# Routing the older chunks of attention sooner, and turning the last chunk's first image later

## The reference

```python
t = _to_tokens(x)
t = t + _L1_attn_ref(_ln_t(t), ...)
t = t + _L1_ffn_ref(_ln_t(t), ...)

# attention, 8 searches of width 16, 2 retrievals
search_attn = softmax(einsum('bsid,bsjd->bsij', sq, sk))
retrieved = einsum('bsij,brjd->bsird', search_attn, rv)
rk = retrieved @ wk_ret
retrieval_attn = softmax(einsum('bsid,bsird->bsir', rq, rk))
out = einsum('bsir,bsird->bsid', retrieval_attn, retrieved)   # then @ w_out

# experts, 8 of them, each token goes to its 2 best
router_logits = einsum('bsd,de->bse', x, Wg)
top_logits, top_idx = top_k(router_logits, 2)
top_w = softmax(top_logits)
out = out + cw[:, e:e + 1] * (silu(xt @ W1[e]) @ W2[e])       # summed over e
```

## Time and profile before

| | |
|---|---|
| runs | 669.68, 670.31, 671.67 us, median 670.31 |
| profiled execution | 670.67 us |
| its span from first to last instruction | 668.9 us |
| PE, DVE, ACT, POOL busy | 565.4, 474.3, 333.6, 262.1 us |
| mean granted clock of PE | 0.924 |

### The profile page before, as it was taken

One profiled execution on the slowest core, in us unless ns is written; L12 is line 12 of the kernel. 1 busy time (PEld: TensorE's weight loads), 2 busy tenths in 40 slices (PEclk: granted clock), 3 DMA queues, 4 the chain that ended last, 5 costly groups with the idle time before them and its releaser, 6 DMA issues. The chain is left out here.

```text
span 668.9 us, 10706 instructions
## 1 busy us (share of the span) xinstructions
PE 565.4 (85%) x3180; PEld 438.6 (66%) x3180; DVE 474.3 (71%) x1227; ACT 333.6 (50%) x718; POOL 262.1 (39%) x328
## 2 busy tenths in 40 slices
PE   5999999939878999999999997884199999999910
PEld 4788888727655776767676765553078888888800
DVE  6796775756467778888888797876357676776716
ACT  3321412124446555565646464552178888888700
POOL 3245344539100010141413232357504666666660
PEclk9999999968969999999999997987579999999975
DMA  8994144649731403142323223001397777786009
GB/s 268 355 371 143 65 159 161 193 159 391 212 110 48 143 16 127 33 132 59 126 65 106 87 87 105 18 32 41 96 340 241 227 242 239 238 248 212 36 9 367
DMA packets 55224, 105.46 MB, mean 158 GB/s; under 512 B 8744, under 2 KB 21689, under 8 KB 55040
## 3 DMA queue, kind: packets, MB, share of 16 engines
q1 hardware_dynamic: 49040, 94.93, 43.0%
q0 software_dynamic: 4992, 8.54, 3.6%
q10 hardware_dynamic: 1136, 1.31, 0.8%
HBM read 58.15 MB, written 48.42 MB: 159 GB/s over the span
## 5 line engine op out<-in xcount | busy, mean ns | idle before, releaser
L1978 POOL DMA_INDIRECT y_slots<-virt,pad_l x92 | 95.9, 1043 | 73.2 <-DVE virt L2030 50.1
L1304 DVE TENSOR_REDUCE s_max<-bank 128x2 f32<-128x512 f32 x128 | 85.9, 687 | 24.3 <-PE bank L1627 23.6
L1069 ACT ACTIVATE s_expd<-bank 128x512 f32<-128x512 f32 x128 | 76.9, 602 | 48.8 <-PE bank L1648 47.8
L983 POOL DMA_INDIRECT x_slots<-rows,slot_of x64 | 62.4, 976 | 67.4 <-DVE rows L1435 49.8
L2018 DVE TENSOR_TENSOR k_stack<-virt,k_stack 128x512 fp32r<-128x512 f32 x92 | 63.5, 690 | 25.5 <-ACT k_stack L1997 24.8
L947 POOL TENSOR_TENSOR ln_rstd<-ln_var,power 128x4 f32<-128x4 f32 x17 | 17.4, 1026 | 146.7 <-DVE ln_var L1280 146.6
L1663 PE MATMUL bank<-s_expd,rvx 128*64 128x256 f32 x512 | 71.7, 402 | 1.6 <-ACT s_expd L1069 1.1
L61 PE MATMUL bank<-pad_h,u_h 128*128 128x512 f32 x144 | 59.4, 412 | 9.4 <-DVE pad_l L399 8.2
L1648 PE MATMUL bank<-q_stack,k_stack 100*128 100x256 f32 x256 | 61.8, 324 | 5.2 <-DVE q_stack L1322 5.0
L1997 ACT ACTIVATE k_stack<-virt 128x512 fp32r<-128x512 f32 x92 | 58.2, 633 | 10.5 <-PE bank L63 8.0
L1992 ACT ACTIVATE virt<-bank 128x512 f32<-128x512 f32 x92 | 55.1, 598 | 14.5 <-PE bank L63 14.3
(11 more groups left out here) (260 smaller groups left out, 1321.2 us busy)
## 6 DMA issues: line engine op xcount, KB each, us to landing
x_slots<-blank SPq DMA_DIRECT2D x8, 2112.0 KB, 17.3
pad_h<-w_split SPq DMA_DIRECT2D x23, 512.0 KB, 4.1
q_stack<-w_split SPq DMA_DIRECT2D x23, 512.0 KB, 5.8
qk_rows<-qk SPq DMA_DIRECT2D x15, 512.0 KB, 3.1
k_stack<-qk_rows SPq DMA_DIRECT2D x96, 64.0 KB, 2.5
pad_l<-x_slots SPq DMA_DIRECT2D x23, 264.0 KB, 5.1
q_stack<-qk_rows SPq DMA_DIRECT2D x42, 128.0 KB, 2.5
e_raw<-in_w SPq DMA_DIRECT2D x16, 256.0 KB, 2.9
```

The costliest lines, as they stand in the source:

```text
L983: pool.indirect_dma_start(out=x_slots[:, :], out_offset=bass.IndirectOffsetOnAxis(ap=slot_of[:, ring, k, j:j + 1], axis=0), in_=rows[:, ri ...
L1069: nc.scalar.activation(expd[:, s % 4].rearrange("p a i -> p (a i)"), ps_st[s % 2][:, :], ACT.Exp).then_inc(exp_done, 1)
L1304: nc.vector.tensor_reduce(s_max[:, :, s], banks[s % len(banks)][:, :].rearrange("p (a j) -> p a j", a=2), AX.X, ALU.max).then_inc(max_done, 1)
L1978: pool.indirect_dma_start(out=y_slots[:, :], out_offset=bass.IndirectOffsetOnAxis(ap=ids, axis=0), in_=y_rows[:, t % 2, j, :], in_offset=N ...
```

## The change

Nothing that is computed changes, only the order of work in the bodies of g = 6 and g = 7. On DVE, the third routing part of chunk 4 and the statistics of chunk 5 go behind the first half of body 6; chunk 4 is ranked and placed within its second half; chunk 5 is routed at the end of it instead of in body 7, and placed in the first half of body 7. Chunk 6 is turned back and routed by PE one head sooner, and routed on DVE between the retrieval parts of the last chunk's image A. PE turns image A at head 7 and makes its output product behind the last retrieval. ACT's copies follow. On POOL, chunk 5's scatters go around the rstd of chunk 6, and three scatters of chunk 6 instead of one go ahead of the rstd of image A.

```diff
 # POOL
         for g in range(1, NCH):
+            if g == NCH - 1:
+                scatter(g - 2, 1, (0,), (0, 1))
             rstd(tail_norm(g - 1))
+            if g == NCH - 1:
+                scatter(g - 2, 1, (0,), (2, 3))
+                scatter(g - 2, 1, (1,))
             copy_rows(g - 1, (g - 1) % 2)
             if g + 2 < NCH:
                 rstd(2 * g + 2)
-            if g >= 2:
+            if g >= 2 and g < NCH - 1:
                 scatter(g - 2, g % 2)
-        scatter(NCH - 2, 0, (0,), (0,))
+        scatter(NCH - 2, 0, (0,), range(0, 3))
         rstd(tail_norm(IMAGE_A))
-        scatter(NCH - 2, 0, (0,), range(1, G))
         pool.wait_ge(scattered[1], 2 * G * 16 * (NCH // 2 - 1))
         number_rows(NCH - 1, 1)
-        scatter(NCH - 2, 0, (1,), (0,))
+        scatter(NCH - 2, 0, (0,), range(3, 4))
+        scatter(NCH - 2, 0, (1,), range(0, 3))
         rstd(tail_norm(IMAGE_B))
-        scatter(NCH - 2, 0, (1,), range(1, G))
+        scatter(NCH - 2, 0, (1,), range(3, 4))
 # ACT, body: share_exp; last_body: share_exp, keep_z2, keep_logits, keep_o
-                    if s == 4 and g >= 2:
+                    if g >= 2 and s == (4 if stage == MIDDLE else 1):
                         share_exp(g - 2)
...
+                if s == 1:
+                    share_exp(g - 2)
                 if s == 2:
                     gate(g - 1, 1)
                 if s == 4:
                     keep_o(g - 1)
-                if s == 6:
-                    share_exp(g - 2)
...
+                if s == 1:
+                    keep_z2(g - 1)
                 if s == 2:
                     gate(g, 0)
-                    keep_z2(g - 1)
-                if s == 4:
                     keep_logits(g - 1, 0)
                 if s == 6:
+                    share_exp(g - 1)
+                if s == 7:
                     keep_o(IMAGE_A)
-                    share_exp(g - 1)
 # DVE, body; R5 = (6, 7)
-                    if s == 6:
+                    if s == 6 and stage == MIDDLE:
                         norm_stats(tail_norm(g - 1), t2_kept, g - 1)
...
-                if g >= 2 and s in (4, 5, 6):
+                if g >= 2 and s in (4, 5, 6) and not (stage == LAST_BUT_ONE and s == 6):
                     route(g - 2, ring, s - 4)
             split_max(g, 1)
             place_max(g, 1, ring, max_bank(stage))
-            if stage in (LAST_BUT_ONE, LAST):
-                normalise_t2(g - 1, 1 - ring)
+            if stage == LAST_BUT_ONE:
+                norm_stats(tail_norm(g - 1), t2_kept, g - 1)
             for s in range(S):
+                if stage == LAST_BUT_ONE and s == 1:
+                    normalise_t2(g - 1, 1 - ring)
...
+                if s == 0 and stage == LAST_BUT_ONE:
+                    route(g - 2, ring, 2)
+                if s == 2 and stage == LAST_BUT_ONE:
+                    place_spots(g - 2)
+                    place_rows(g - 2, ring)
                 if s == 1:
                     retrieve(g, 0, 0)
-                if s == 4:
+                if s == (4 if ahead else 3):
                     retrieve(g, 0, 1)
-                if s == 5:
+                if s == (5 if ahead else 4):
                     retrieve(g, 0, 2)
-                if g >= 2 and s == 7:
+                if stage == MIDDLE and g >= 2 and s == 7:
                     place_spots(g - 2)
+                if stage == LAST_BUT_ONE and s in R5:
+                    route(g - 1, 1 - ring, R5.index(s))
...
-            if g >= 2:
+            if stage == MIDDLE and g >= 2:
                 place_rows(g - 2, ring)
+            if stage == LAST_BUT_ONE:
+                for part in range(len(R5), 3):
+                    route(g - 1, 1 - ring, part)
 # DVE, last_body
-                if s in (1, 2, 3):
+                if s in (1, 2):
                     retrieve(g - 1, 1, s - 1)
-                if s == 5:
+                if s == 2:
+                    retrieve(g - 1, 1, 2)
+                if s == 3:
+                    place_spots(g - 2, ps_conv)
+                    place_rows(g - 2, ring)
+                if s == 4:
                     add_attention(g - 1)
-                if s == 6:
                     norm_stats(tail_norm(g - 1), t2_kept, g - 1)
-                if s in (2, 3, 4):
-                    route(g - 2, ring, s - 2)
...
             normalise_t2(g - 1, 0)
-            place_spots(g - 2)
-            place_rows(g - 2, ring)
-            for part in range(3):
-                retrieve(g, 0, part)
+            retrieve(g, 0, 0)
             for part in range(3):
                 route(g - 1, 0, part)
+            retrieve(g, 0, 1)
+            retrieve(g, 0, 2)
             place_spots(g - 1)
             place_rows(g - 1, 0)
             add_attention(IMAGE_A)
 # PE, body
-                    if s == 2:
+                    if s == (2 if stage == MIDDLE else 3):
                         tail_turn_back(g - 1, 1 - ring)
...
-                if g >= 2 and s == 6:
+                if stage == LAST_BUT_ONE and s == 1:
+                    pe.wait_ge(t2_kept, g)
+                    rank(g - 2)
+                if stage == MIDDLE and g >= 2 and s == 6:
                     rank(g - 2)
 # PE, last_body
+                if s == 1:
+                    pe.wait_ge(logits_kept, g - 1)
+                    rank(g - 2, ps_conv)
...
             retrieve(g, 0, NP - 1, ring)
-            pe.wait_ge(t2_kept, g)
-            rank(g - 2)
-            pe.wait_ge(logits_kept, g - 1)
+            pe.wait_ge(spot_read, 4 * (g - 2) + 1)
             turn_max(g, 1, ps_conv)
...
+                if s == 1:
+                    tail_turn_back(g - 1, 0)
                 if s == 2:
-                    tail_turn_back(g - 1, 0)
-                if s == 3:
                     tail_route(g - 1)
-                if s == 5:
-                    tail_turn(IMAGE_A)
                 if s == 6:
+                    pe.wait_ge(t2_kept, g)
                     rank(g - 1)
                 if s == 7:
-                    tail_out(IMAGE_A)
+                    tail_turn(IMAGE_A)
             retrieve(g, 1, NP - 1, ring)
+            tail_out(IMAGE_A)
```

More of the change, by code:

```diff
@@ L1435, in place_rows @@
             nc.vector.tensor_tensor(share[:, 1], share[:, 0], gap_e[:, at], ALU.mult).then_inc(rows_ready, 1)
+        R5 = (6, 7)
         def body(g, ring, stage):
+            ahead = stage in (FIRST, MIDDLE)
             for s in range(S):
```

## The result

The changed kernel takes 671.95 us (median of 18 runs, 669.21 to 674.62), the kernel before 670.33 (18 runs, 668.09 to 671.67). The ratio is 1.0025, with a 95% interval of 1.0013 to 1.0037: 1.6 us slower, clear of noise, though under the 0.3% that I called the limit of what can be told. Forecast were 668.1 and a range of 666.5 to 670.3. Both the sign and the range were wrong.

A forecast was written before the change was run, and what follows sets the result against it. Attention's last scatter bounds the experts' start, set by POOL's queue and DVE's order ending together. Of 3.4 us won by DVE and PE, three scatters cost 1.2, leaving 2.2: 668.1 us from a 670.31 median, range 666.5 to 670.3.

The forecast's parts named there:

- Half 6.1: First half of body 6: DVE loses chunk 5's statistics and chunk 4's third routing part, 2.12 us shorter.
- Half 6.2: Second half of body 6: DVE's pieces 14.5 plus 2.2 us, PE's clock staying up; 1.1 of 2.1 won given back.
- Half 7.1: First half of body 7: DVE's 11.5 plus 0.3 plus 2.2 us, so 7.2 begins at 439.5, 2.9 sooner.
- the addition at head 4: In 7.1, DVE's addition of the attention output waits for PE's output product: 0.3 us, at most 1.0.
- the clock here as a rival: PE's clock falls in 7.1 for 3.4 us, costing 1.0; gain 0.2 to 1.4, about 669.3 us; chance 0.20.
- Half 7.2: Second half of body 7: chunk 6's rows ready 10.9 us in, at 450.4 against 455.03.
- both sides agreed: In 7.2, DVE's order (10.4 plus 0.3 for POOL's copy) and PE's ranking (10.0 plus placing, 11.0) gave similar times.
- the rival of the whole lead: Chunk 6's routing not held, PE at full clock in 7.2: tail moves 3.1 to 3.6, 667.0 us; chance 0.12.
- POOL's order: Three scatters of chunk 6 ahead of A's rstd, not one, cost 1.2 of the 3.4 us DVE and PE win.
- A's rstd behind three scatters decides, slower: Tail: if chunk 6's rows come after 452.6, loses; ranking no sooner normalises A 2.4 late, 672.7 us; chance 0.10.
- Forecast A: Start of image A's first scatter on POOL, forecast at 468.0 instead of 470.20, 2.2 us sooner.
- three signs: Signs of error: 7.1 clock under 0.9, over 1 us DVE idle in 6.2, chunk 6's ranking past 10 us into 7.2.

The follow-up runs named there:

- run 1: Changed kernel with 21 idle-time PE products (128x512, results unread) around the turnings ending 6.1, 6.2 and 7.1: 666.82 us, ratio 0.9957 to the kernel before.
- run 5: Changed kernel with idle-time PE products only around the turning that ends 6.2 (5 ahead, 4 behind): 669.39 us, ratio 0.9995 to the kernel before.
- run 10: Changed kernel with idle-time PE products, POOL's old order, chunk 6's addition back at head 5 and statistics at head 6: 665.25 us, ratio 0.9930.
- run 4: Kernel before with only POOL's new order, three scatters of chunk 6 ahead of image A's rstd: 672.40 us, ratio 1.0041.
- run 2: Changed kernel with POOL's old order, one scatter of chunk 6 ahead of image A's rstd: 669.87 us, ratio 1.0007 to the kernel before.
- run 7: Changed kernel with idle-time PE products at all three half ends and POOL's old order: 666.24 us, ratio 0.9943 to the kernel before.
- run 11: Changed kernel with chunk 5's second routing part moved behind the placing of 7.1's maxima: 672.71 us, ratio 1.0032 to the kernel before.
- run 6: Changed kernel with DVE's addition of chunk 6 and its statistics back at heads 5 and 6 of 7.1: 671.00 us, ratio 1.0023.
- run 9: Changed kernel with 21 idle-time PE products at the three half ends, each 8 columns instead of 512: 673.29 us, ratio 1.0035.
- run 12: Changed kernel with idle-time PE products, POOL's old order, later addition, and chunk 5's second routing part behind the turning: 665.49 us, ratio 0.9934.
- run 8: Changed kernel with idle-time PE products, POOL's old order, and 24 more products behind attention's last small product: 666.56 us, ratio 0.9950.

## Why the prediction was wrong, step by step

**Half 6.1: right.** 2.12 forecast, 2.13 measured.

**Half 6.2: the step that failed first.** The prediction says: "The fall came behind the idle 2.65 and 0.96 us; the first of these shrinks to 0.5, so I take the clock to stay up." It shrank to 0.53 and the clock fell as far as before (0.81 against 0.79). The sum of DVE's pieces was good: 16.7 forecast, 16.37 with the clock held. The 1.3 between that and 17.68 are the low clock, which makes PE late with the scores.

**Half 7.1: the step that cost most.** 14.0 forecast, 17.54 measured. 2.8 are the clock (run 1, and run 5 with that fall alone), 1.0 the addition at head 4, for which I had charged 0.3 (run 10). With both taken away it is 13.77: the terms from the earlier trace rows were sound. I had the clock here as a rival, at a chance of 0.20 and a price of 1.0. The mechanism was the right one and its price wrong. I took the shortest low stretch that the trace had, 3.4 us, as the case, and it lasted 6.7, about as in 6.2 of the earlier trace rows (6.5), for which I allowed "up to 2". I let PE's slack in that half cover a part of it, where DVE's maxima, its addition and, through ACT behind PE's retrieval, its gate all wait for PE. And the argument against a fall, that the 1.88 us stand "cost no clock", rested on one execution: in run 4's the same stand in the same code was followed by one. The figures of that rival do not follow from each other either: a loss of 0 to 2 leaves a gain of 0.2 to 2.2, and a loss of 1.0 gives 669.1, not "about 669.3"; it changes nothing here.

The Trainium skill's remark on small idle times (TensorE: Matmul & The Clock Gate, A second HAM failure mode) pointed to this rival, and the runs agree: 0.81 with the gaps, 1.00 with them filled. I had laid it to the many short waits inside 6.2; run 5 leaves those as they are, fills only the stand around the turning, and 7.1 keeps its clock (1.00).

**Half 7.2: right on DVE's side.** Chunk 6's rows were ready 10.9 us in, as forecast. That both sides agreed was luck: PE reached the ranking at 451.49, 8.3 in and not 10.0, with its clock at 1.00, and DVE's order alone set the time. The copy of POOL held one step of DVE from 0.19 to 0.59, 0.4 where I charged 0.3. That the clock stays up there (1.00, before 0.88) was half forecast, in the rival of the whole lead. The Trainium skill's rule on two-input steps (GPSIMD Engine Reference, Specifications) is borne out: the copy ran from 447.63 to 448.26, and the one such step that lay over it ended at 448.32. The next began at 448.36, behind the copy, and took 0.21. What I drew from the rule was wrong: the steps in a queue cannot each be held by one copy that the first outlasts.

**POOL's order: right in kind.** It was forecast to eat 1.2 of the lead; taken back, it gives 1.3 (run 2) and 1.4 (run 7) in the profiles. The rival "A's rstd behind three scatters decides, slower" had as its condition that chunk 6's rows come less than 2.4 us sooner than now. From the common point they came 0.1 sooner (454.05 - 391.10 = 62.95 against 455.03 - 391.94 = 63.09), because of the two halves above. So the slower case is this rival with the clock as its cause: I had priced them apart, and they came together. A normalised then stands at 68.41 against 66.45, 2.0 late, of the 2.4 that I gave for it.

**The sum.** Forecast A 2.2 us sooner, measured 1.9 later: 4.1 apart, which is what run 1 gives back in the profile (80.13 to 76.04). That run is also, at 666.82, in the range that I gave. That it lands on the forecast A to a few hundredths (76.04 against 76.06) is in part luck: its 7.2 begins 0.5 later from the common point than forecast, and the way from there to A is 0.5 shorter (28.0 against 28.5). Two of the three signs that I had named as making the forecast wrong were there: a clock under 0.9 in 7.1, and more than 1 us of DVE idle in 6.2 (17.68 - 14.97 = 2.7).

What stays open is when a gap brings a fall, and how often. The stand of 1.88 us in 7.1 brought none in the profile of the kernel before and one in run 4's; 0.96 and a few short waits in run 11 did. So it is shown that filled gaps keep the clock and give the time back. That the new order makes a fall in 7.1 more frequent rests on few executions: all four profiles with that order and no large products in the gaps have one (the changed kernel, runs 2, 6 and 9), and one of two with the old order (run 4, and not the kernel before).

## What to carry to other kernels

Where an engine paces a half and PE waits for it, PE's clock is a term of the sum and not a condition: price each half at both levels before moving work, with the longest low stretch that the trace shows (even that was exceeded in run 11), and do not take a clock that one profile shows as kept for one that every execution keeps. A few unused products in PE's standing times are a cheap test of it, and here they were worth more (0.3% on the kernel before, 0.7% on the changed one) than the reordering. They are fitted to one gap, though: where the gap goes, as in run 12, they hold up the work behind them. And when a wait moves one head forward in an engine's queue, its price is what stands behind it, which here was the maximum that PE's next scores needed.

## What the runs showed of the hardware

- 21 products of 512 columns in the gaps hold the granted clock at 1.00 in 6.2 and 7.1 (run 1); the same number of products of 8 columns in the same places leave it at 0.81 (run 9).
- The same stand of 1.88 or 1.87 us in the same code left the clock at 1.00 in one execution (the kernel before) and was followed by 0.50 in another (run 4).
- Work that ended at 478.25 did not carry the clock to 484: 0.93 in the mean of 478 to 482, 0.50 from 482 on (run 8).
- A copy of 128x512 on POOL (0.63 us) held one DVE step of two SBUF inputs for 0.4 us (0.59 instead of 0.19), to just behind the copy's end. The two-input step behind it took 0.21, with POOL's two small copies of 128x4 running.
